# Attention of 8-wide heads: a third pair of score banks once the maxima are done, and the rows of maxima turned behind the values

## The reference

```python
# stage 4 (no mask); stage 10 adds a relative bias before the scale, and masks
att = jnp.einsum('bhid,bhjd->bhij', q, k) / math.sqrt(D)      # D = 8
att = jnp.einsum('bhid,bhjd->bhij', q, k) + bias[None]        # stage 10
att = jnp.where(causal[None, None], att * (1.0 / math.sqrt(D)), -jnp.inf)
att = jax.nn.softmax(att, axis=-1)
y = jnp.einsum('bhij,bhjd->bhid', att, v)
```

## Time and profile before

| | us |
|---|---|
| three timed runs | 3409.17, 3416.59, 3417.78 |
| their median | 3416.59 |
| the profiled execution | 3408.68 |
| its span | 3406.9 |
| PE busy in it | 3023.7 (89%) |
| DVE busy | 2440.1 (72%) |
| ACT busy | 1802.7 (53%) |
| POOL busy | 851.4 (25%) |

### The profile page before, as it was taken

One profiled execution on the slowest core, in us unless ns is written; L12 is line 12 of the kernel. 1 busy time (PEld: TensorE's weight loads), 2 busy tenths in 40 slices (PEclk: granted clock), 3 DMA queues, 4 the chain that ended last, 5 costly groups with the idle time before them and its releaser, 6 DMA issues. The chain is left out here.

```text
span 3406.9 us, 61884 instructions
## 1 busy us (share of the span) xinstructions
PE 3023.7 (89%) x24429; PEld 1641.8 (48%) x24469; DVE 2440.1 (72%) x5485; ACT 1802.7 (53%) x3298; POOL 851.4 (25%) x809
## 2 busy tenths in 40 slices
PE   4878679998799999998899989798998898898999
PEld 3435456666322222223566657476775222333677
DVE  8898688777699999994877743745336888884433
ACT  2223347777477777775778743133222466776211
POOL 0333147765100000002966700101203111212000
PEclk8898889999699999999999989898999699998899
DMA  1065221110420000001211110002002300000100
GB/s 54 9 160 138 64 64 34 37 37 11 153 81 2 1 1 1 1 1 28 63 28 35 31 31 1 12 18 75 25 1 83 103 32 1 35 2 1 48 1 13
DMA packets 77879, 129.20 MB, mean 38 GB/s; under 512 B 12772, under 2 KB 52616, under 8 KB 77384
## 3 DMA queue, kind: packets, MB, share of 16 engines
q1 hardware_dynamic: 77592, 125.25, 13.0%
HBM read 77.39 MB, written 34.19 MB: 33 GB/s over the span
## 5 line engine op out<-in xcount | busy, mean ns | idle before, releaser
L2039 ACT ACTIVATE AR<-ps 128x1024 f32<-128x1024 f32 (+2 forms) x756 | 717.7, 995 | 275.3 <-PE ps L1940 207.9
L2126 DVE TENSOR_REDUCE AR<-ps 128x1 f32<-128x512 f32 x1296 | 808.4, 682 | 43.0 <-PE ps L1909 42.0
L1940 PE MATMUL ps<-AR 32*128 32x512 bf16 (+3 forms) x4992 | 536.0, 378 | 6.4 <-ACT AR L2039 4.2
L1909 PE MATMUL ps<-AR 32*128 32x512 bf16 (+3 forms) x1664 | 478.1, 398 | 41.3 <-DVE AR L2126 13.7
L1957 PE MATMUL ps<-AR 128*32 128x512 f32 (+3 forms) x3328 | 439.8, 602 | 4.9 <-ACT AR L2044 3.1
L2535 PEld LDWEIGHTS ps<-AR 128*128 128x128 f32 x3072 | 362.9, 192 | 60.5 <-issue 47.5
L2694 DVE SCALAR_TENSOR_TENSOR X<-ps,AR,X 128x128 f32<-128x128 f32 x512 | 143.6, 344 | 343.5 <-PE ps L2535 343.2
L1909 PEld LDWEIGHTS ps<-AR 32*128 32x128 bf16 x1664 | 120.1, 92 | 548.5 <-DVE AR L2126 410.3
L2535 PE MATMUL ps<-AR 128*128 128x128 f32 x3072 | 363.0, 275 | 0.0
L2510 PE MATMUL ps<-XT,AR 128*128 128x512 f32 x672 | 307.7, 594 | 0.1
L205 POOL TENSOR_TENSOR rs<-rs,halves 128x4 f32<-128x4 f32 x48 | 49.5, 1031 | 841.7 <-DVE rs L197 841.7
(11 more groups left out here) (326 smaller groups left out, 5004.2 us busy)
## 6 DMA issues: line engine op xcount, KB each, us to landing
AR<-AR SPq DMA_DIRECT2D x124, 128.0 KB, 2.3
band<-AR SPq DMA_DIRECT2D x32, 450.0 KB, 5.1
AR<-band SPq DMA_DIRECT2D x32, 448.0 KB, 5.1
AR<-in_c_rot SPq DMA_DIRECT2D x64, 128.0 KB, 2.2
AR<-in_L3f_w SPq DMA_DIRECT2D x30, 256.0 KB, 5.6
rows_KA<-AR SPq DMA_DIRECT2D x32, 128.0 KB, 2.4
AR<-scr_bias SPq DMA_DIRECT2D x32, 128.0 KB, 3.1
AR<-in_L2f_w SPq DMA_DIRECT2D x30, 128.0 KB, 2.9
```

The source lines that it names most:

```text
L1909: e.matmul(g.bank[b][:, 0:w], QA[rows, q, 128 * i:128 * i + 128], KA[rows, q, 512 * first:512 * first + w], start=way != "kept", stop=True ...
L1940: t = e.matmul(g.bank[h][:, lo:512], K[32 * h:32 * h + 32, q, 128 * kt:128 * kt + 128], Q[32 * h:32 * h + 32, q, queries], start=y == 0, s ...
L2039: e.activation(dst[:, :, lo:512], src[:, :, lo:512], ACT.Exp, scale=self.scale).then_inc(*s.up("exp" if u else "left", k, i, *((1,) if u e ...
L2126: e.tensor_reduce(o, g.bank[b][:, 0:w], AXX, ALU.max).then_inc(*s.up("reduced", k, n, h, st, kc))
```

## The change

There are four edits, all in `Attn8`.

1. In `lay_plan`, the turn moves from in front of the finish and the values to behind the values of its step.
2. From the first step at which all 16 rounds are closed and turned (`free_from`: step 238 in stage 4, 139 in stage 10), scores go around three pairs, (0, 1), (2, 3), (5, 6), half after half; `base[i, u]` notes the first bank of a half. The ring shrinks to bank 7, which only finishes use then.
3. From that step on values wait for the second exp of their own step, since no score in front of them does so any more.
4. PE, ACT and DVE take the pair from `base` in place of a fixed one.

The work itself, its sizes and its count are unchanged.

```diff
+        self.base, self.free_from, pairs_used = {}, None, 0
...
+            if self.closed == 16 and not self.rows_due and self.free_from is None:
+                self.free_from, self.banks = i, (7,)
             for u in range(2):
                 for x in slots[u]:
                     self.plan_max(*x)
-                self.plan.append(("score", i, n, kt, u, self.hold(2 * u, ("exp", i, 1) if u else ("left", i)) + self.hold(2 * u + 1)))
+                b = 2 * u
+                if self.free_from is not None:
+                    b = (0, 2, 5)[pairs_used % 3]
+                    pairs_used += 1
+                self.base[i, u] = b
+                self.plan.append(("score", i, n, kt, u, self.hold(b, ("exp", i, 1) if u else ("left", i)) + self.hold(b + 1)))
             self.plan.append(("step", i, n, kt))
             for x in slots[2]:
                 self.plan_max(*x)
-            if self.rows_due:
-                self.plan_rows_max(self.rows_due.pop(0))
             if finish_due and min(self.done) == len(units):
                 self.plan_finish(finish_due.pop(0))
...
                 self.plan.append(("values", i - 1, pn, pk))
                 if pk == last_kt[pn]:
                     finish_due.append(pn)
+            if self.rows_due:
+                self.plan_rows_max(self.rows_due.pop(0))
...
                 if self.near_cols(n, kt):
                     e.wait_ge(*s.at("exp", k, i, 0))
-                elif i == len(self.steps) - 1:
+                elif i >= self.free_from or i == len(self.steps) - 1:
                     e.wait_ge(*s.at("exp", k, i, 1))
```

More of the change, by code:

```diff
@@ L1939, in tensor @@
                     for h in (2 * u, 2 * u + 1):
-                        t = e.matmul(g.bank[h][:, lo:512], K[32 * h:32 * h + 32, q, 128 * kt:128 * kt + 128],
+                        t = e.matmul(g.bank[self.base[i, u] + h % 2][:, lo:512], K[32 * h:32 * h + 32, q, 128 * kt:128 * kt + 128],
                                      Q[32 * h:32 * h + 32, q, queries], start=y == 0, stop=y == 2, skip_group_check=True)
@@ L2022, in scalar @@
                 for u in range(2):
-                    src = g.ps[:, 1024 * u:1024 * u + 1024].rearrange("p (a b) -> p a b", a=2)
+                    src = g.ps[:, 512 * self.base[i, u]:512 * self.base[i, u] + 1024].rearrange("p (a b) -> p a b", a=2)
                     dst = self.PB[:, (2 * kt + u) % 4, :].rearrange("p (a b) -> p a b", a=2)
@@ L2136, in vector @@
                 (gr, qc), (a, z) = self.rounds[n], self.near_cols(n, kt)
-                y = g.ps[:, 1024:2048].rearrange("p (a b) -> p a b", a=2)[:, :, a - 512 * qc:z - 512 * qc]
+                b = self.base[i, 1]
+                y = g.ps[:, 512 * b:512 * b + 1024].rearrange("p (a b) -> p a b", a=2)[:, :, a - 512 * qc:z - 512 * qc]
                 e.wait_ge(*s.at("scored", k, i, 1))
```

## The result

The changed kernel takes 3393.10 us (median; runs 3391.10, 3391.64, 3394.56, 3395.09) beside 3415.95 us for the kernel before (3409.17, 3415.31, 3416.59, 3417.78). The ratio is 0.9938, 95% interval 0.9925 to 0.995: 22.8 us less, between 17 and 26. The profiled execution took 3391.10 us (span 3389.3), 17.6 us less than the profiled one of before, where the sum said 18.1.

What follows compares the result with a forecast made beforehand. DVE was taken to bound stage 4's body, PE and ACT handing banks to and fro the tails. Stage 4's 8.6 and stage 10's 9.5 make 18.1 us off the median 3416.59: 3398 given, range 3385 to 3410.

Steps and rivals of the forecast that it cites:

- The turn, stage 4: Body of stage 4: next maxima go 0.28 us earlier at each of 14 turns, 3.9 us; 0.3 for the fifteenth.
- The pairs, tail of stage 4: 13 steps at PE's pace of 2.36 us save 2.8 us; four steps without a finish, 1.90 each, save 1.6.
- The added wait: Tails: values waiting for their own second exp cost nothing with a finish; at 0.06 us for 39 values, 2.3 less gain.
- The turns, stage 10: Body of stage 10: two places at 1.0 us and 2.0 over the others, 4.0; seven turns counted as lost.
- The last turn, stage 10: Scores of step 138 to those of 139: 2.99 us in place of 4.19, saving 1.2.
- The stretch of 16.56 us: Tail of stage 10, three pairs: 1.2 us back, mostly in steps 148 to 150.
- The stretch of 11.58 us: Tail of stage 10: 0.3 us for DVE's early bias and 0.9 for ACT's stop at 3128.97, together 1.2.
- The last stretch, 10.88 us: End of stage 10's tail, clock granted 0.56: scores of step 158 earlier by 0.3 to 1.6 us, taken as 1.0.
- the turn gives nothing: Rival, chance 0.17: third max, ACT's copy and three-bank ring set DVE's stop; 9.9 us gained in all, 3407.
- the pairs are not used: Rival, chance 0.10: in-order PE runs ahead by less than a pair, tails stay at 2.58 us a step; 3407.
- More than I count: Rival, chance 0.12: all DVE's stop goes in stage 4, stage 10's copies come earlier, clock stays up; 29.2 us, 3387.
- The clock falls in the tails: Rival, chance 0.06: granted clock drops in the tail steps; half of them slow costs 40 us more, 3438.

Runs made afterwards that it cites:

- wait only: The kernel before with only the values' added wait for their own step's second exp, in the tails: 3419.79 us in its one run, beside 3412.44 for the kernel before.
- turn only: The kernel before with the turn moved behind the values and nothing else: 3400.18 us, ratio 0.9962 to the kernel before.
- pairs only: The changed kernel with the turn put back in front of the finish and values, three pairs kept in the tails: 3403.47 us, ratio 0.9974 to the kernel before.

## Why the prediction was right, step by step

- **The turn, stage 4.** 14 x 0.28 = 3.9 was predicted, 4.06 (4.01, 3.84) measured, and 0.25 for 0.3 at the last one. The row arithmetic held in each part: 0.31 us from max to values, 1.00 for the values, 0.54 for the turn, and ACT's copy over at 1458.43 for 1458.34. The upper bound of 11.6 was far: the rest of DVE's stop, 0.54 us a turn, stays.
- **The pairs, tail of stage 4.** 2.8 and 1.6 predicted, 2.88 and 1.51 measured. The loop of the last steps ran at 1.93 us a step, not 1.90.
- **The added wait** costs 0.00 us in the steps with a finish, as argued from the extra wait at 1549.32; wait only shows it. The count of 39 values was too high: 24 got a new wait.
- **The turns, stage 10.** 4.0 predicted. The first profiles of the two kernels differ by 2.27 us, but the second of before lies 3.85 over its first. Four profiles of the body in before's order (435.80, 439.65, 443.92, 443.99) have a mean of 440.8, five in the changed order (433.52, 436.98, 433.61, 437.10, 436.50) one of 435.5: 5.3 less, clock included. At equal clock I find 0.89 + 0.71 + 0.90 at the turns 49, 70 and 127, about 2.5 us, and next to nothing elsewhere. The reason given for the lost ones, ACT's place for the copy, is borne out for 0.3 to 0.5 us at three turns and open for the rest. The two places at 1.0 came out as two at 0.9; the 2.0 "over the others" were too much, they were one place at 0.7.
- **The last turn, stage 10:** 1.2 predicted, 1.10 measured. **Steps 139 to 143:** 0.9 and 0.97. **The stretch of 16.56 us:** 1.2 and 1.13.
- **The stretch of 11.58 us:** 1.2 predicted, 0.73 measured, of which 0.24 is the clock (0.98 to 1.00; turn only and wait only have the same 0.24 without the pairs). The change's share is 0.49: this term was mis-sized. The 0.9 of it was taken from ACT's stop at 3128.97, which lies behind the end of the stretch (3127.47). Inside it ACT's stops were these before, and these after:

```profile
3116.76 0.39 ACT L2029 ACTIVATE AR<-ps 128x256 f32<-128x256 f32 x1 [0.42 <-PE ps L1940]
3120.41 1.02 ACT L2039 ACTIVATE AR<-ps 128x1024 f32<-128x1024 f32 x1 [0.32 <-DVE ps L2139]
3122.92 0.81 ACT L2039 ACTIVATE AR<-ps 128x768 f32<-128x768 f32 x1 [0.21 <-DVE ps L2139]
3125.07 0.60 ACT L2039 ACTIVATE AR<-ps 128x512 f32<-128x512 f32 x1 [0.31 <-DVE ps L2139]
3125.96 0.63 ACT L2044 ACTIVATE AR<-AR 128x512 f32<-128x512 f32 x1 [0.29 <-POOL AR L2196]
```

```profile
3103.78 0.39 ACT L2037 ACTIVATE AR<-ps 128x256 f32<-128x256 f32 x1 [0.41 <-PE ps L1948]
3110.18 0.63 ACT L2052 ACTIVATE AR<-AR 128x512 f32<-128x512 f32 x1 [0.23 <-POOL AR L2205]
3112.50 0.63 ACT L2052 ACTIVATE AR<-AR 128x512 f32<-128x512 f32 x1 [0.72 <-POOL AR L2205]
```

  The pairs took away the 0.84 us that ACT stood for DVE's bias, and the waits for POOL grew from 0.29 to 0.95 in their place.
- **The last stretch, 10.88 us:** 1.0 predicted; from step 156 to 159, which lies in it, 2.71 measured, and the step failed all the same. Wait only has 2.70 of it with neither edit. It is the granted clock, and the share of the change is near zero: pairs only and turn only, at 0.80 and 0.79, took 8.37 and 8.22 us. The prediction took 1.0 for the pairs here and no change of clock. The 0.9 to 1.1 us less behind step 159 is the same clock (1.05 in wait only).
- **Sum and median.** Stage 4 gave 8.7 us for 8.6, stage 10 with what follows it 10.0 for 9.5 (of which 3.8, the last stretch and the end, are the clock's), the rest of the program took 1.2 more. Profile against profile 17.6 stands for 18.1, and that it is so near is in part luck. What can be put down to the edits at equal clock is 8.7 in stage 4 and 2.5 + 1.1 + 0.97 + 1.13 + 0.49 = 6.2 in stage 10, 14.9 us in all; the clock gave some 4 more at the end of stage 10, and the rest of the program took 1.2 back. The median fell by 22.8, 4.7 more than the sum; on another chip it fell by 22.4. The first profile of before had the fastest body of stage 10 of four, by 3.9 to 8.2 us. That fits a profiled execution near the low end of its runs. The mean clock of each run points the same way: of the 15 runs of before on one chip, those under 3410 us had 0.933 to 0.936, those over 3416 had 0.929 to 0.933. In which stage the runs without a profile lost it wasn't seen, so the 4.7 us stay argued.

Of the rivals, *the turn gives nothing* falls by turn only, *the pairs are not used* by pairs only. *More than I count* came near by the number, not by its mechanism: DVE's stop went by a third only. *The clock falls in the tails* is false in every stretch of the tails up to step 159 in the three profiles of the changed kernel, where it stayed or rose. The rule of the Trainium skill beside that rival (TensorE: Matmul & The Clock Gate, "A second HAM failure mode: psum-queue depth-cycling") finds no support in the tail of stage 4 either, now cycling three pairs at 1.00.

## What to carry to other kernels

When an in-order engine has independent work behind a wait, count the time from the last thing the waiter needs to the next thing it is fed, in rows of the trace: the gain is that difference and not the whole stop. Then ask who frees the buffer that comes third, and where its release stands in *its* engine's list; here moving it one instruction ahead was worth 0.3 to 0.5 us at each of three turns. And take a second profile of the kernel before: a stretch whose granted clock is between the levels isn't a base from which tenths can be read.

## What the runs showed of the hardware that I had not expected

The body of stage 10 took 433.5 to 444.0 us over the nine profiles in before's and the changed order, 2.4%, while the tails repeated within 0.06 us from profile to profile of one kernel. The difference lies mostly in places of one to six steps where the granted clock is low (0.65 over the three steps above) in one kernel and 1.00 in another, for the same instructions in that part. The place at steps 134 to 136 kept its value in the two and three profiles of a kernel and differed between kernels with the same instructions in that part (before and wait only). An edit of 1 or 2 us there can't be told from what the clock does by the time alone, only step by step at equal clock.
